# Two of sixteen tiles' neighbour coordinates by indirect DMA on GpSimd in place of lookups by matrix product

## The chip, the cores and the metric

The kernel runs on one core of a Trainium2 chip. The metric is the device time of one execution in microseconds (us), the median of several runs.

## What is computed

There are B = 2 samples with N = 1024 points. Each point has C = 512 features in `x` and 1024 coordinates in `ctx`. Two layers follow each other.

```python
# layer 0: 8 nearest neighbours in ctx, four blocks (w_center = w_neighbor = w = fside)
idx = top_k(-squared_distance(ctx), 8)
for i in range(4):
    shortcut = points
    p = leaky_relu(points, 0.01)
    g = gather(p, idx)
    points = (w[i] @ p + (w[i] @ g).sum(neighbours)) / 9 + shortcut
# layer 1: 30 nearest neighbours in ctx, features from the first three coordinates only
idx = top_k(-squared_distance(ctx), 30)
rel = ctx[first three][idx] - ctx[first three][own]
feat = spherical(rel), and the same less its mean           # 6 per neighbour
h = lrelu(bn(feat @ W1.T)); h = lrelu(bn(h @ W2.T)); h = lrelu(bn(h @ W3.T))   # 6, 3, 1
att = softmax(h, over 30 neighbours)
out = x + sum_k att[k] * x[idx[k]]
```

`bn` normalises with the mean and the variance over all points of both samples, so no point of layer 1 is through it before the coordinates of the neighbours of all 2048 points are there.

## The kernel before

**Tiles and passes.** The 2048 points are 16 tiles (`TILES`) of 128; tiles 0 to 7 are the first sample. The four blocks of layer 0 are eight passes, `it` = 0 to 7, the samples in turn. A pass has sixteen steps, numbered through as g = 16 it + s. Steps 0 to 7 are the aggregation half: a unit of work (`aggregate`, L1447 to L1468) is 16 matmuls of 128x512, adjacency `nbr` against the high and the low part of the features. The first two units of a pass are issued together, their matmuls alternating (a double step), and both end with it. Steps 8 to 15 are the product half (`wp`, L1470 to L1490), 12 matmuls each, with the weights `wT` in a high and a low part.

**What stands behind a unit.** Each aggregation unit leaves a bank that ACT copies (`q_high`, L719) and from which DVE makes the low part (`q_low`, L994). PE wants the low part of a unit before the third one behind it, since there are three banks (`s_ql`). Each product step is added to `X` by DVE (`x_update`, L1000). GpSimd (POOL in the profile) makes the next pass's features in product steps: `p_join` (L496) and `p_low` (L501). In pass 2 it also makes four low parts of the second half of the weights (`w_low`, L460), which the product half of pass 2 waits for.

**Order.** Each engine has a program of its own. PE, ACT and DVE do, after their part of step g, what `side(g)` has for it; GpSimd has a loop of its own over the same steps (L547 to L571), without a wait for the step itself. Layer 1 lies in these places:

- `SEL_AT`: the selection of the 30 neighbours on DVE, to step 43 (pass 2). It leaves `idx`, the neighbours' numbers. Tiles 0 and 1 are the first and stand ahead of pass 0.
- `ROWS_AT` = steps 30, 33, 36, 44: `index_rows` (L1004 to L1013), four small DVE operations that split the numbers of four tiles into a row and a place in it. PE turns them, and SP writes them to DRAM and reads them back broadcast over 128 partitions, one DMA for each lookup (L380 to L397).
- Lookups, from `G0` = 44: a lookup `u` is 15 neighbours of the 128 points of a tile, so 32 in all, two in a step. DVE and ACT turn the broadcast numbers into one-hots (L1017, L732), PE multiplies them with a table of coordinates in three bf16 parts (`lookup`, L1500 to L1515: 45 matmuls of 128x24), and DVE's `pick_r` (L1020 to L1031) takes the wanted one of eight in each group of 24 and writes it to `near`. They lie in steps 45 to 61 on PE.
- `NET_AT`: 47 steps of the small network from `M0` = G0 + TILES + 2 = 62 on, mostly DVE and ACT over all 61,440 neighbours at once. In some of them PE sums statistics over the partitions (L1519).
- `T0` = 109: the attention weights are turned (L1241 to L1245 on DVE make their parts). From `S0` = T0 + 6 = 115 on DVE makes one-hots (`onehots`, L1257 and L1266), and PE multiplies them two times a step into rows of a 128 x 1024 matrix of weights (`spread`, L1573, 64-column matmuls), the first one ahead of the unit of step S0 + 1. `S_END` of these 32 spreads lie inside pass 7; the others, and the weighted sum itself (`attend`, L1612 to L1614), come behind it.

On SP the own-coordinate loads (L360) take single elements: 1024 of them for a coordinate of a sample.

## Time and profile before

| | |
|---|---|
| median of 3 runs | 716.52 us (716.1 to 717.33) |
| the profiled execution | 717.41 us |
| its span in the trace | 715.7 us, so 1.7 us outside |
| PE busy | 699.1 us (98% of the span) |
| DVE busy | 576.3 us (81%) |
| ACT busy | 347.9 us (49%) |
| GpSimd busy | 249.9 us (35%) |
| granted TensorE clock, mean | 0.995 of full speed |

Matmuls are pipelined: a row gives 0.39 us for a large one though the next starts 0.227 us later. So a busy share of 98% does not say that PE is at its best; distances between starts do. The trace gives times from the start of the span. A row of a timeline has the start, the duration, the engine, the line, the operation with its operands, how many like it follow each other, and, in brackets, how long the engine stood idle before and what released it.

### The profile page before, as it was taken

What the parts mean: (1) busy time and instruction counts of PE and PEld (TensorE: products, weight loads), DVE (VectorE), ACT (ScalarE), POOL (GpSimd) and SP (SyncE); (2) the same over time, 40 slices, a digit from 0 to 9 for tenths busy, and PEclk for the clock granted to TensorE, in tenths of its full rate; (3) what the DMA queues carried; (4) which work ended last, traced back from release to release, by engine and by line L of the source; (5) the groups of instructions that cost most, each with busy time, mean ns of one, the idle gap of its engine ahead of it and who ended that gap; (6) DMA issues with size and microseconds to landing.
All of it is one profiled execution on the core that took longest, in us unless ns stands there. A gap on an engine that the chain in (4) does not pass through costs nothing.

```text
span 715.7 us, 13026 instructions
## 1 busy us (share of the span) xinstructions
PE 699.1 (98%) x5458; PEld 584.2 (82%) x5458; DVE 576.3 (81%) x848; ACT 347.9 (49%) x526; POOL 249.9 (35%) x216
## 2 busy tenths in 40 slices
PE   5999999999999999999999999999999999999998
PEld 4799889778888887888888888877887887888887
DVE  4699999999699899766789798677686799678831
ACT  6456646448517137767892263384463244223210
POOL 2258757656608327300165083065074000000000
PEclk9999999999999999999999999999999999999999
DMA  8510301100000103645510000000000000100101
GB/s 350 182 3 1 117 1 37 53 29 1 1 1 0 62 24 141 200 154 163 179 38 1 1 0 1 0 1 1 0 1 0 2 1 2 45 32 32 45 30 60
DMA packets 21564, 35.66 MB, mean 50 GB/s; under 512 B 10113, under 2 KB 10369, under 8 KB 21505
## 3 DMA queue, kind: packets, MB, share of 16 engines
q1 hardware_dynamic: 20976, 33.78, 14.2%
q10 hardware_dynamic: 528, 1.05, 0.4%
q8 instruction: 43, 0.70, 0.4%
q14 instruction: 17, 0.13, 0.1%
HBM read 30.50 MB, written 4.33 MB: 49 GB/s over the span
## 4 chain that ended last, share of the span: by engine, by line
PE 81%; DVE 9%; POOL 4%; ACT 3%; issue 1%; DMA 1%; SPq 0%; POOLq 0%; DVEq 0%
PE bank L1464 27%; PE bank L1486 7%; PE bank L1488 6%; PE bank L1487 6%; PE bank L1511 5%; PE bank L1573 4%; PE bank L1612 4%; PE bank L1614 4%; PE bank L1375 4%; PE bank L1613 4%; PE bank L1377 4%; PE bank L1376 4%; DVE idx L967 2%; DVE vals L965 2%; POOL pts_l L430 1%
## 5 line engine op out<-in xcount | busy, mean ns | idle before, releaser
L1464 PE MATMUL bank<-nbr,pts_h 128*128 128x512 f32 x512 | 202.7, 396 | 1.5 <-DVE pts_l L994 1.4
L1464 PE MATMUL bank<-nbr,pts_l 128*128 128x512 f32 x512 | 200.0, 391 | 0.0
L496 POOL TENSOR_TENSOR p_second<-p_first,p_second 128x512 f32<-128x512 f32 x58 | 76.9, 1329 | 196.9 <-ACT p_second L706 196.9
L1464 PEld LDWEIGHTS bank<-nbr,pts_h 128*128 128x128 f32 x512 | 96.6, 189 | 23.1 <-issue 2.1
L719 ACT CAST pts_h<-bank 128x512 fp32r<-128x512 f32 x64 | 37.1, 587 | 159.4 <-PE bank L1464 159.2
L1464 PEld LDWEIGHTS bank<-nbr,pts_l 128*128 128x128 f32 x512 | 96.6, 189 | 19.7 <-issue 0.2
L1486 PE MATMUL bank<-wT,pts_h 128*128 128x512 f32 x256 | 102.2, 399 | 0.0
L1488 PE MATMUL bank<-wT,pts_l 128*128 128x512 f32 x256 | 100.3, 392 | 0.0
L1487 PE MATMUL bank<-wT,pts_h 128*128 128x512 f32 x256 | 100.1, 391 | 0.0
L994 DVE TENSOR_TENSOR pts_l<-bank,pts_h 128x512 fp32r<-128x512 f32 x64 | 44.0, 688 | 48.8 <-ACT pts_h L719 48.4
L501 POOL TENSOR_TENSOR pts_l<-p_second,pts_h 128x512 fp32r<-128x512 f32 x58 | 78.3, 1356 | 2.0 <-ACT pts_h L712 2.0
L1375 PE MATMUL bank<-pts_h 128*128 128x512 f32 (+3 forms) x192 | 68.8, 358 | 8.8 <-DVE pts_l L927 8.3
L837 ACT CAST nbr<-bank 128x512 fp32r<-128x512 f32 x64 | 35.2, 590 | 78.3 <-PE bank L1573 78.3
L1376 PE MATMUL bank<-pts_l,pts_h 128*128 128x512 f32 (+3 forms) x192 | 66.1, 344 | 0.0
L1377 PE MATMUL bank<-pts_h,pts_l 128*128 128x512 f32 (+3 forms) x192 | 66.1, 344 | 0.0
L1488 PEld LDWEIGHTS bank<-wT,pts_l 128*128 128x128 f32 x256 | 48.3, 189 | 10.3
L1486 PEld LDWEIGHTS bank<-wT,pts_h 128*128 128x128 f32 x256 | 48.5, 189 | 9.5
L1487 PEld LDWEIGHTS bank<-wT,pts_h 128*128 128x128 f32 x256 | 48.5, 189 | 9.5
L712 ACT CAST pts_h<-p_second 128x512 fp32r<-128x512 f32 x58 | 35.7, 616 | 31.2 <-POOL p_second L496 31.2
L1000 DVE SCALAR_TENSOR_TENSOR X<-bank,X 128x512 f32<-128x512 f32 x64 | 43.9, 689 | 7.8 <-PE bank L1488 7.2
L1612 PE MATMUL bank<-pts_h,nbr 128*128 128x512 f32 x120 | 48.7, 406 | 0.6 <-DVE pts_l L1275 0.6
L1375 PEld LDWEIGHTS bank<-pts_h 128*128 128x128 f32 x192 | 36.6, 191 | 13.7 <-issue 7.3
(212 smaller groups left out, 1338.4 us busy)
## 6 DMA issues: line engine op xcount, KB each, us to landing
more<-a_rows SPq DMA_DIRECT2D x17, 480.0 KB, 4.5
scratch<-a_rows SPq DMA_DIRECT2D x15, 480.0 KB, 4.7
X<-in_ctx SPq DMA_DIRECT2D x12, 512.0 KB, 6.1
out_dram<-X SPq DMA_DIRECT2D x15, 256.0 KB, 2.0
more<-in_ctx SPq DMA_DIRECT2D x4, 512.0 KB, 5.6
X<-in_x SPq DMA_DIRECT2D x2, 1024.0 KB, 5.2
X<-in_x SPq DMA_DIRECT2D x1, 1536.0 KB, 7.0
w_raw<-in_fside_BxSxS SPq DMA_DIRECT2D x1, 1024.0 KB, 11.5
```

The source lines that it names most:

```text
L496: pool.tensor_tensor(p, a, b, ALU.subtract).then_inc(s_p32, 1)
L501: pool.tensor_tensor(p_l[:, m, :], parts(n)[2], p_h[:, m, :].bitcast(F32), ALU.subtract).then_inc(s_p1, 1)
L994: dve.tensor_tensor(q_l[:, j, :], bank[g % 3][:], q_h[:, j, :].bitcast(F32), ALU.subtract).then_inc(s_ql, 1)
L1000: dve.scalar_tensor_tensor(dst, bank[3 + g % 3][:], 1.0 / (K0 + 1.0), dst, ALU.mult, ALU.add).then_inc(s_xu, 1)
L1375: pe.matmul(o, pts_h[:, k, rows], pts_h[:, k, cols], start=(k == 0), stop=False)
L1376: pe.matmul(o, pts_h[:, k, rows], pts_l[:, k, cols], start=False, stop=False)
L1377: return pe.matmul(o, pts_l[:, k, rows], pts_h[:, k, cols], start=False, stop=(k == KT - 1))
L1464: mm = pe.matmul(bank[u % 3][:], p[:, m, t * P:(t + 1) * P], nbr[b][:, m, hf * HALF:(hf + 1) * HALF], start=(m == 0 and part_ == 0), stop= ...
L1486: pe.matmul(bank[3 + g % 3][:], q_h[:, q, cols], wT[:, hi, t, :], start=(t == 0), stop=False)
L1487: pe.matmul(bank[3 + g % 3][:], q_h[:, q, cols], wT[:, 1 - hi, t, :], start=False, stop=False)
L1488: mm = pe.matmul(bank[3 + g % 3][:], q_l[:, q, cols], wT[:, hi, t, :], start=False, stop=(t == CT - 1))
L1612: pe.matmul(o, lhs[0], rhs[0], start=(r == 0), stop=False)
```

## The change

`GATHERED_TILES` = 2. The coordinates of the neighbours of tiles 0 and 1 no longer come from lookups. Three DMAs on SP write the first three coordinates of the first sample into a DRAM table of 1024 rows, point by point. GpSimd then issues 60 indirect DMAs, one for each tile and neighbour: each reads 128 numbers from `idx` and fetches 128 rows of three coordinates into `near_rows`. `GATHER_AT` places them in the first halves of passes 1, 2 and 3: 16, 16 and 28. Ahead of the network's first step DVE waits for all 60 and copies them into `near`.

28 lookups stay, those of tiles 2 to 15, still two a step from step 45 on. Since `M0` follows their number, the network starts at step 60 and not 62, `T0` is 107 and `S0` 113, and four more spreads lie inside pass 7 (`S_END` 30 and not 26).

```diff
+    GATHERED_TILES = 2
+        near_rows = sb("near_rows", [P, GATHERED_TILES, K1, 3], F32)
+        tab_d = nc.dram_tensor("table", [N, 3], F32, kind="Internal").ap()
+        GT = GATHERED_TILES
+        LOOKUPS = 2 * (TILES - GT)
...
-        M0 = G0 + TILES + 2
+        M0 = G0 + LOOKUPS // 2 + 2
+        GATHER_AT = {16: 2, 17: 2, 18: 2, 19: 2, 20: 2, 21: 2, 22: 2, 23: 2, 32: 3, 33: 3, 34: 3, 35: 3, 36: 1, 37: 1, 38: 1,
+                     39: 1, 48: 4, 49: 4, 50: 4, 51: 4, 52: 3, 53: 3, 54: 3, 55: 3}
...
+            for j in range(3):
+                sp.dma_start(tab_d[:, j].unsqueeze(1), ctx[0, 2 - j, :].unsqueeze(1),
+                             allow_slow_non_contiguous=True).then_inc(s_tabd, 16)
...
             for c in range(CHUNKS):
-                for t in range(2 * CH):
-                    u = 2 * CH * c + t
+                for t in range(2 * CH) if c else range(2 * GT, 2 * CH):
+                    u = 2 * CH * c + t - 2 * GT
...
+                    done = sum(GATHER_AT[q] for q in GATHER_AT if q < g)
+                    for i in range(done, done + GATHER_AT.get(g, 0)):
+                        if i == 0:
+                            pool.wait_ge(s_tabd, 16 * 3)
+                            pool.wait_ge(s_sel, GT)
+                        pool.indirect_dma_start(
+                            out=near_rows[:, i // K1, i % K1, :], out_offset=None, in_=tab_d,
+                            in_offset=bass.IndirectOffsetOnAxis(ap=idx[:, i // K1, i % K1:i % K1 + 1], axis=0)) \
+                            .then_inc(s_rows, 16)
...
-                if 0 <= g - G0 < TILES:
+                if 0 <= g - G0 < LOOKUPS // 2:
                     onehot_a(2 * (g - G0) + 1)
...
             def pick_r(u):
-                T, k0 = u // 2, (u % 2) * KH
+                T, k0 = GT + u // 2, (u % 2) * KH
...
                 if n == 0:
+                    dve.wait_ge(s_rows, 16 * GT * K1)
+                    link(dve.tensor_copy(near[:, :, 0:GT, :], near_rows[:].rearrange("p t k j -> p j t k")))
...
-                    if 0 <= u < 2 * TILES:
+                    if 0 <= u < LOOKUPS:
...
-                b = u // (2 * NT)
+                b = (GT + u // 2) // NT
```

What moves on GpSimd in passes 1 and 2. Before, the four low parts of the weights (L460) of pass 2 stand right behind the features made in pass 1 (L496, L501; `x2` means two in a row):

```order
L496 TENSOR_TENSOR p_second<-p_first,p_second 128x512
L501 TENSOR_TENSOR pts_l<-p_second,pts_h 128x512 x2
L460 TENSOR_TENSOR wT<-w_raw,wT 128x512 x4
L496 TENSOR_TENSOR p_second<-p_first,p_second 128x512 x2
L501 TENSOR_TENSOR pts_l<-p_second,pts_h 128x512
```

With the change (L511 and L516 are the features, L475 the low parts):

```order
L511 TENSOR_TENSOR p_second<-p_first,p_second 128x512
L516 TENSOR_TENSOR pts_l<-p_second,pts_h 128x512 x2
L579 DMA near_rows<-table,idx 128x3 x12
L475 TENSOR_TENSOR wT<-w_raw,wT 128x512
L579 DMA near_rows<-table,idx 128x3
L475 TENSOR_TENSOR wT<-w_raw,wT 128x512
L579 DMA near_rows<-table,idx 128x3
L475 TENSOR_TENSOR wT<-w_raw,wT 128x512
L579 DMA near_rows<-table,idx 128x3
L475 TENSOR_TENSOR wT<-w_raw,wT 128x512
L579 DMA near_rows<-table,idx 128x3
L511 TENSOR_TENSOR p_second<-p_first,p_second 128x512 x2
```

Twelve gathers now stand ahead of the first low part of the weights, and one behind each of the four.

What moves on DVE at the passes 6 and 7. Before, the parts of the turned weights (L1241 to L1245) end ahead of pass 7, three low parts of its aggregation (`q_low`, L994) follow, and then one-hots 0 (L1257 twice, L1266):

```order
L1241 CAST more<-scratch 128x512x2
L1242 TENSOR_TENSOR more<-scratch,more 128x512x2
L1243 TENSOR_TENSOR scratch<-bank,scratch 128x512
L1244 CAST more<-scratch 128x512x2
L1245 TENSOR_TENSOR more<-scratch,more 128x512x2
L994 TENSOR_TENSOR pts_l<-bank,pts_h 128x512 x3
L1257 TENSOR_TENSOR scratch<-scratch 128x512
L1257 TENSOR_TENSOR scratch<-idx,scratch 128x2048
L1266 TENSOR_TENSOR scratch<-scratch,more 128x2048
L994 TENSOR_TENSOR pts_l<-bank,pts_h 128x512
```

With the change (L1267 to L1271 the parts, L1024 the product steps of pass 6, L1018 `q_low`, L1283 and L1292 one-hots 0):

```order
L1267 CAST more<-scratch 128x512x2
L1268 TENSOR_TENSOR more<-scratch,more 128x512x2
L1269 TENSOR_TENSOR scratch<-bank,scratch 128x512
L1270 CAST more<-scratch 128x512x2
L1271 TENSOR_TENSOR more<-scratch,more 128x512x2
L1024 SCALAR_TENSOR_TENSOR X<-bank,X 128x512 x2
L1018 TENSOR_TENSOR pts_l<-bank,pts_h 128x512
L1283 TENSOR_TENSOR scratch<-scratch 128x512
L1283 TENSOR_TENSOR scratch<-idx,scratch 128x2048
L1292 TENSOR_TENSOR scratch<-scratch,more 128x2048
L1018 TENSOR_TENSOR pts_l<-bank,pts_h 128x512
```

The parts now end two product steps ahead of pass 7, and one-hots 0 stand behind its first low part and not its third; on PE the first spread stands behind the double step of pass 7 and ahead of its third unit.

## Rows read from the trace of the kernel before

**Rows 1.** The page, chain that ended last: share of the span by engine.
```profile
PE 81%; DVE 9%; POOL 4%; ACT 3%; issue 1%; DMA 1%; SPq 0%; POOLq 0%; DVEq 0%
```
**Rows 2.** The chain in order of time: start us, us, engine, line and count.
```profile
352.08 2.27 PE bank L1511 x90
357.19 2.27 PE bank L1511 x90
...
433.80 29.03 PE bank L1464 x128
```
**Rows 3.** Own-coordinate loads: SP's queue in the timeline; the page's DMA issues (landing).
```profile
38.58 0.43 SPq L360 DMA_DIRECT2D own<-in_ctx  x1
...
own<-in_ctx SPq DMA_DIRECT2D x6, 4.0 KB, 2.3
```
**Rows 4.** Timeline of GpSimd, passes 1 to 3.
```profile
218.04 2.56 POOL L496 TENSOR_TENSOR p_second<-p_first,p_second 128x512 f32<-128x512 f32 x2 [25.66 <-ACT p_second L706]
...
235.60 2.54 POOL L501 TENSOR_TENSOR pts_l<-p_second,pts_h 128x512 fp32r<-128x512 f32 x2
254.07 1.29 POOL L460 TENSOR_TENSOR wT<-w_raw,wT 128x512 fp32r<-128x512 f32 x1 [15.92 <-ACT wT L579]
...
265.09 1.29 POOL L460 TENSOR_TENSOR wT<-w_raw,wT 128x512 fp32r<-128x512 f32 x1 [2.43 <-ACT wT L579]
...
352.36 1.27 POOL L496 TENSOR_TENSOR p_second<-p_first,p_second 128x512 f32<-128x512 f32 x1 [53.72 <-ACT p_second L706]
```
**Rows 5.** Timeline of PE: the first normalisation sum, and the start of pass 6.
```profile
471.49 0.39 PE L1519 MATMUL bank<-stat,mean_mat 128*128 128x12 f32 x2 [0.52 <-DVE stat L1073]
...
490.66 0.39 PE L1464 MATMUL bank<-nbr,pts_l 128*128 128x512 f32 x1
...
492.63 0.40 PE L1464 MATMUL bank<-nbr,pts_l 128*128 128x512 f32 x1
```
**Rows 6.** Timelines of ACT, DVE and PE at the start of pass 7.
```profile
545.70 1.08 ACT L719 CAST pts_h<-bank 128x512 fp32r<-128x512 f32 x2 [3.57 <-PE bank L1464]
549.78 0.59 ACT L719 CAST pts_h<-bank 128x512 fp32r<-128x512 f32 x1 [3.00 <-PE bank L1464]
...
550.40 0.69 DVE L994 TENSOR_TENSOR pts_l<-bank,pts_h 128x512 fp32r<-128x512 f32 x1 [1.40 <-ACT pts_h L719]
...
553.80 0.39 PE L1573 MATMUL bank<-scratch 128*128 128x64 bf16 x8 [0.43 <-issue]
```
**Rows 7.** Timeline of PE: an idle in pass 0, and matmuls in pass 2.
```profile
146.70 0.47 PE L1464 MATMUL bank<-nbr,pts_h 128*128 128x512 f32 x1 [1.44 <-DVE pts_l L994]
...
288.19 0.63 PE L1487 MATMUL bank<-wT,pts_h 128*128 128x512 f32 x1
288.62 0.63 PE L1488 MATMUL bank<-wT,pts_l 128*128 128x512 f32 x1
```
**Rows 8.** Busy us of each engine (operations) by windows; granted clock; DMA share; GB/s.
```profile
283.40:287.00 3.60, 2.27 (x70) 1.84 (x69) 3.60 (x6) 2.50 (x3) 1.33 (x2) 1.00 0.99 370
287.00:290.40 3.40, 3.40 (x36) 2.82 (x33) 3.23 (x8) 3.40 (x5) 0.82 (x1) 0.50 0.90 285
...
310.90:314.30 3.40, 3.40 (x49) 2.92 (x46) 3.23 (x8) 3.37 (x3) 0.00 (x0) 0.50 0.83 260
```
**Rows 9.** Timeline of DVE in pass 2: index rows, a `q_low`, a one-hot.
```profile
237.04 1.19 DVE L1009 TENSOR_SCALAR scratch<-idx 128x128 uint32<-128x128 uint32 x1
...
245.50 0.69 DVE L994 TENSOR_TENSOR pts_l<-bank,pts_h 128x512 fp32r<-128x512 f32 x1 [1.83 <-ACT pts_h L719]
...
249.69 0.22 DVE L1009 TENSOR_SCALAR scratch<-idx 128x128 uint32<-128x128 uint32 x1
...
282.23 1.36 DVE L1012 CAST scratch<-scratch 128x128 bf16<-128x128 uint32 x1
283.51 1.74 DVE L1017 TENSOR_SCALAR scratch<-scratch,part 128x1920 bf16<-128x1920 bf16 x1
```
**Rows 10.** Timeline of PE: the first product matmul of pass 2.
```profile
267.30 0.39 PE L1486 MATMUL bank<-wT,pts_h 128*128 128x512 f32 x1
```

More of the change, by code:

```diff
@@ L249, in build @@
         s_tab = sem("table_ready")
+        s_tabd = sem("table_stored")
+        s_rows = sem("neighbour_rows_landed")
         s_first = sem("first_term_ready")
@@ L389, in _ @@
                         sp.dma_start(a_rows[CHUNKS - 1], a_row[:]).then_inc(s_arow, 16)
-                    if u == 2 * CH * (CHUNKS - 1):
+                    if u == 2 * CH * (CHUNKS - 1) - 2 * GT:
                         sp.wait_ge(s_arow, 16 * CHUNKS)
@@ L1282, in side @@
                     index_rows(ROWS_AT[g])
-                if 0 <= g - G0 < TILES:
+                if 0 <= g - G0 < LOOKUPS // 2:
                     onehot_a(2 * (g - G0))
                 for u in (2 * (g - G0) - 4, 2 * (g - G0) - 3):
-                    if 0 <= u < 2 * TILES:
+                    if 0 <= u < LOOKUPS:
                         pick_r(u)
@@ L1529, in side @@
                 for u in (2 * (g - G0) - 2, 2 * (g - G0) - 1):
-                    if 0 <= u < 2 * TILES:
+                    if 0 <= u < LOOKUPS:
                         lookup(u)
```

## Prediction

> **What bounds the kernel now.** I read the chain that ended last first: PE holds 81% of it [rows 1]. Then I read PE's own timeline, where the reader should look at the distances between starts and not at the busy shares. Large matmuls start 0.227 us apart nearly everywhere: 29.03 us for the 128 of an aggregation half [rows 2], so 3.63 us for an aggregation step of sixteen and 2.72 us for a product step of twelve. Behind the selection PE is the bound and rarely waits; what leaves its queue is a gain, and what makes it idle is a loss that nothing later repays. The exceptions are therefore what matters: the start of the lookups (283 to 314 us), the normalisation sums (471 and 491 us) and the first spread (553.8 us).
>
> **What is removed.** Four of 32 lookups, two steps with two each. A pair of lookups is 90 small matmuls in 2.27 us, and product steps that carry one start 5.11 us apart, from 352.08 to 357.19 [rows 2], against 2.72 without. Steps 60 and 61, both product steps, lose it: 2 x (5.11 - 2.72) = **4.8 us less on PE**, straight on the bound. ACT, DVE and SP lose the one-hots, reads and broadcasts of these lookups; none of them is on the bound there, so I count nothing.
>
> **What is added on queues.** Three table stores on SP: the nearest row is the own-coordinate load, also 1024 single elements, 0.43 us to issue and 2.3 us to land [rows 3]. They stand right behind those loads, and the reader is GpSimd at 192 us (218.04 less 25.66 [rows 4]): nothing. Sixty gathers on GpSimd: no row shows one. From below it is an issue of 0.43 us, from above a full landing, 2.3 us [rows 3]; I take 1.3 us, what GpSimd needs for one of its own operations (two in 2.54 us at 235.60 [rows 4]), since both are work over 128 rows on that engine. GpSimd does not wait for the steps of the table, so each batch begins when its queue is free. Pass 1: 16 x 1.3 = 20.8 us into an idle stretch of 25.66 us that ends at 218.04. Pass 2: 12 x 1.3 = 15.6 us into 15.92 us, before the first low weight part at 254.07, then one gather after each of the four parts, which start 3.7 us apart (254.07 to 265.09) and take 1.3. Pass 3: 28 x 1.3 = 36.4 us into 53.72 us [rows 4]. All fits, barely in pass 2, and costs nothing as long as a gather is no dearer. The copy of 180 elements on DVE at step 60 lies where PE does not wait for DVE: nothing.
>
> The Trainium skill (DMA: Bandwidth & Descriptors, Latency and other measured facts) gives about 1 us to the first byte of a DMA issued from GpSimd; no run shows one here yet. By that page twelve would be an estimated 12 us, and the sum is the same.
>
> **What is moved.** The network, the turning of the weights and the spreads all start two steps earlier.
>
> First the two waits that the network now causes. At 471.49 PE stood 0.52 us for the first sum's statistics, in the third product step of pass 5, behind a backlog of DVE work that does not fit 2.72 us steps. At 490.66 to 492.63, the start of pass 6, six starts took 1.97 us where 1.36 would do: 0.6 us for late low parts, since six normalisations on ACT held them up [rows 5]. Two steps earlier the heavy items before the sum fall in aggregation steps of 3.6 us, and the normalisations come before more of the product half: I take both waits as gone, **-1.1 us**. New ones of the same kind may appear (the second sum now follows the pass's double step, and the weights' parts are made beside the low parts of pass 7): 0 to 1 us, **+0.5 us**, by the 0.52 and 0.6 of these rows.
>
> Then the first spread, the term that decides. Before, one-hots 0 stand on DVE three `q_low` into pass 7 and PE wants them after four aggregation units; PE idled 0.43 us [rows 6]. Now they stand after the first `q_low`, and PE wants them right behind the double step that opens the pass. In that double step the two units alternate and end together, so no unit of work lies between. From the copy on ACT that follows a unit to the spread it took 553.80 - 549.78 = 4.02 us (copy, then 3.40 us from `q_low` through the one-hots [rows 6]). The copy after the double step started at 545.70, so the spread could start at 549.72; PE is through with the pair two matmuls after that copy is released, at 546.15. Idle 3.6 us in place of 0.43: **+3.1 us**, and nothing behind it has room to give it back.
>
> Does the clock fall in such a hole? It stayed at full speed after the one idle of 1.44 us at 146.70: the matmul behind it took 0.47 us, and not the 0.63 of those at the lower level [rows 7]. It was granted 0.50, the 1.2 GHz level, for 3.4 us twice, at 287.0 after 3.6 us of waiting and small matmuls, and at 310.9 [rows 8]; large matmuls then started 0.43 us apart, 288.19 to 288.62 [rows 7]. 3.6 us of pure idle is nearer to the second kind. 3.4 us hold eight matmuls at 0.2 us extra each, 1.6 us; a part falls on the spread's small ones: **+1.4 us**, with 0 and 1.7 as ends.
>
> **The sum.** -4.8 - 1.1 + 0.5 + 3.1 + 1.4 = -0.9 us on the profiled execution's 717.41, so 716.5 us. That execution is 0.9 us above the median of the runs, 716.52; I carry the difference over to the median: **715.6 us**, -0.13%. A measurement of this kernel can tell about 0.2%, 1.4 us, from no change.
>
> **Rivals.**
>
> 1. *Gathers hold up DVE (slower).* GpSimd's operations do hold up some of DVE's: the shift at 237.04 took 1.19 us, 0.22 us at 249.69 when GpSimd was idle [rows 9]; the selection's searches show nothing of the kind. If a gather does the same, the index rows suffer. They are chains of four small operations, and in the gap between two the next gather starts. At 238 us three of them wait 1.3 us each, 3.9, of which the idle 1.83 us at 245.50 [rows 9] takes back all but 2.1. The second chain then starts at 251.8, and the batch runs to about 254: two waits, 2.6. The third may meet a low part and a gather, 0 to 2.5. DVE has no idle from 245.50 until it starts the lookups, so this moves PE's wait there: 4.7 to 7.2 us, less 1 to 2 if the present collisions (1.36 us for a cast at 282.23, 1.74 for the one-hot behind it [rows 9]) fall away. I take +3: **718.6 us**; the ends are 1 (gathers of 0.8 us) and 6. It is slower than before from 0.9 us up, more than the measurement's grain from 2.3. Against it: a gather reads 128 indices and may hold the memory port shortly. The Trainium skill (SBUF — State Buffer, SBUF: two separate sides) calls the port pair that DVE and GpSimd share an exclusive lock, held for a whole instruction, and says that GpSimd writes its descriptors through it; the slow shift agrees for arithmetic, no run shows a gather.
>
> 2. *The clock holds (faster).* Without the fall and without new small waits: -4.8 - 1.1 + 3.1 = -2.8, **713.7 us**. For it: the idle of 146.70 passed without one. Against: this one is two and a half times as long.
>
> 3. *The hole is not there (faster).* If DVE had one-hots 0 ready in time: -4.8 - 1.1 + 0.5 = -5.4, **711.1 us**. The order of the queue speaks against it.
>
> 4. *The gathers don't fit, so that they are not hidden as meant.* At 2.3 us the twelve of pass 2 end near 266, 11.7 us after the first low weight part was due, and the product that needs the last one starts at 267.30 [rows 10]: PE late by 10 us, **726 us** or more. It begins to cost above about 1.6 us a gather.
>
> **How the numbers follow.** Forecast 0.42, rival 1 0.33, rival 2 0.14, rival 3 0.05, rival 4 0.06. Range 712.9 to 720.0: it leaves out rivals 3 and 4 and the dear end of rival 1 (0.05), together 0.16. Faster by over 0.2% (below 715.1): 0.11 of the forecast, whose terms are good to about 1 us, 0.13 of rival 2, 0.05 of rival 3, 0.01 of rival 1: 0.30. Slower by over 0.2% (above 718.0): 0.20 of rival 1, 0.06 of rival 4, 0.01 of the forecast: 0.27. Within: 0.43.
>
> **What the profile of the changed kernel would show.** Product steps 60 and 61 start 2.72 us apart. Before the first 64-column matmul of pass 7 PE idles some 3.6 us, and the granted clock is 0.50 for a few us behind it; if it is not, rival 2. PE's waits at the first sum and at the start of pass 6 are gone. Index rows in pass 2 take 0.9 us a chain as now; if their operations take over 1 us each and the first lookup starts later against the step's other work, rival 1. GpSimd's gathers end before 254 and leave the low weight parts where they are; otherwise rival 4. Wrong would be above all a hole at the first spread that is shorter than 2 us, or a first lookup more than 1 us later.

## The result: 3.3% slower, and where the time went

The changed kernel takes 739.41 us in the median of 5 runs (739.12 to 743.68), the kernel before 716.79 us beside it: 1.0329 of its time, 95% interval 1.0311 to 1.0346, so 22.6 us slower. The forecast was 715.6 us. The profiled execution is the longest of the five, 743.68 us with a span of 741.9, and the table below is made on it; its mean granted clock is 0.972, that of the four others 0.975 to 0.977.

The chain of the changed kernel, by engine, shows the first sign. "issue", time in which an engine waits for nothing that the profile shows, was 1% in [rows 1]:

```profile
PE 80%; DVE 9%; POOL 4%; issue 4%; ACT 2%; DMA 1%; POOLq 0%; SPq 0%
```

The second view to make is a table by half passes: the distance in PE's timeline from the first large matmul of one half to that of the next, in us. Halves that are not listed agree within 0.04 us.

| half | before | after |
|---|---|---|
| pass 2, product | 31.84 | 30.51 |
| pass 3, aggregation | 49.97 | 76.93 |
| pass 3, product | 33.76 | 29.00 |
| pass 5, product | 22.79 | 22.01 |
| pass 6, aggregation | 29.89 | 29.86 |
| pass 7, aggregation | 34.43 | 42.96 |
| pass 7, product, and the end | 142.64 | 140.49 |

So 27.0 us more in one half, and about what was forecast in the others. (Pass 2's 1.3 us is the clock: before, it fell there [rows 8], this time not.) In pass 3 GpSimd's 28 gathers run from 299.35 to 340.77 us, the first four from beside the large matmuls of the double step, most of the others beside lookups. From their timeline; they start 1.25 us apart, and behind every seventh GpSimd pauses:

```profile
311.07 0.95 POOL L579 DMA_INDIRECT near_rows<-table,idx  x1 [0.30 <-issue]
312.32 0.94 POOL L579 DMA_INDIRECT near_rows<-table,idx  x1 [0.30 <-issue]
315.19 0.95 POOL L579 DMA_INDIRECT near_rows<-table,idx  x1 [1.93 <-issue]
...
339.83 0.94 POOL L579 DMA_INDIRECT near_rows<-table,idx  x1 [0.30 <-issue]
```

And PE's timeline beside them (the small matmuls of the lookups, the number behind x, and in brackets the idle time before):

```profile
305.05 1.29 PE L1537 MATMUL bank<-tab_p,more 128*128 128x24 bf16 x45
306.19 0.27 PE L1537 MATMUL bank<-tab_p,scratch 128*128 128x24 bf16 x5
306.84 0.29 PE L1537 MATMUL bank<-tab_p,scratch 128*128 128x24 bf16 x5 [0.38 <-issue]
307.62 0.25 PE L1537 MATMUL bank<-tab_p,scratch 128*128 128x24 bf16 x4 [0.49 <-issue]
309.05 0.28 PE L1537 MATMUL bank<-tab_p,scratch 128*128 128x24 bf16 x5 [1.18 <-issue]
...
314.82 1.30 PE L1537 MATMUL bank<-tab_p,scratch 128*128 128x24 bf16 x38 [0.52 <-issue]
316.56 0.31 PE L1537 MATMUL bank<-tab_p,scratch 128*128 128x24 bf16 x5 [0.44 <-issue]
...
348.30 2.43 PE L1537 MATMUL bank<-tab_p,more 128*128 128x24 bf16 x90
```

Fifty matmuls run at full pace. Then they come in handfuls, some 0.72 us or twice that from one to the next, in the middle of a lookup: its 45 matmuls wait for semaphores only ahead of the first. At the end of GpSimd's pause (between the rows of 312.32 and 315.19) 38 run freely, and then it starts again. After the last gather a pair takes 2.3 us as in [rows 2]. Behind these gaps the granted clock was 0.50 for a time (the third figure from the end of these rows):

```profile
314.80:316.20 1.40, 1.30 (x38) 1.15 (x37) 0.80 (x2) 0.00 (x0) 0.95 (x1) 0.50 0.72 244
327.70:333.30 5.60, 5.60 (x16) 4.44 (x16) 0.00 (x0) 0.00 (x0) 4.08 (x6) 0.50 0.08 16
```

The lower clock does not make the handfuls, since the 38 free ones ran at it, in 1.30 us. Piece by piece against the same half of the kernel before: the four lookups behind the double step take 22.66 us (305.05 to 327.71) where they took 5.36, the unit behind them 6.37 for 4.88, the next pair of lookups 8.35 (334.08 to 342.43) for 2.28, and the unit behind that 5.87 for 3.74. 17.3 + 1.5 + 6.1 + 2.1 is the 27.0 us; the two units are longer by the clock. One line of the waits from 299 to 342 us sums it up: who waited, for whom, us in total, times, longest. Before:

```profile
PE bank L1511 <- issue: 0.2, 1, 0.2
```

After:

```profile
PE bank L1537 <- issue: 18.5, 30, 1.2
```

The first spread of pass 7, which answers to [rows 6], and the window behind it, with a granted clock of 0.50, which answers to [rows 8]:

```profile
570.33 1.01 PE L1599 MATMUL bank<-scratch 128*128 128x64 bf16 x16 [3.58 <-issue]
571.15 0.77 PE L1490 MATMUL bank<-nbr,pts_h 128*128 128x512 f32 x1
```

```profile
568.90:575.70 6.80, 5.37 (x27) 4.43 (x28) 4.53 (x6) 0.59 (x1) 0.00 (x0) 0.50 0.00 0
```

And the first normalisation sum, [rows 5], now without an idle ahead of it:

```profile
486.11 0.29 PE L1545 MATMUL bank<-stat,mean_mat 128*128 128x12 f32 x2
```

### The profile page after: what moved, and what is told of

It reads as the page before. It is cut to its first block, busy times and chain, and to the rows that moved or that the text cites. A ratio compares the mean times of both kernels' runs of the same rounds, so it can differ in the third digit from the quotient of the medians.

```text
span 741.9 us, 12697 instructions
## 1 busy us (share of the span) xinstructions
PE 705.4 (95%) x5278; PEld 586.8 (79%) x5278; DVE 571.7 (77%) x835; ACT 341.1 (46%) x522; POOL 309.0 (42%) x276
## 4 chain that ended last, share of the span: by engine, by line
PE 80%; DVE 9%; POOL 4%; issue 4%; ACT 2%; DMA 1%; POOLq 0%; SPq 0%
PE bank L1490 27%; PE bank L1512 6%; PE bank L1514 6%; PE bank L1513 6%; PE bank L1537 5%; PE bank L1599 4%; PE bank L1638 4%; PE bank L1640 4%; PE bank L1401 4%; PE bank L1639 4%; PE bank L1403 4%; PE bank L1402 4%; DVE idx L991 2%; DVE vals L989 2%; POOL pts_l L445 1%
## 5 line engine op out<-in xcount | busy, mean ns | idle before, releaser
L1490 PE MATMUL bank<-nbr,pts_h 128*128 128x512 f32 x512 | 206.6, 403 | 1.7 <-DVE pts_l L1018 1.5
L1490 PE MATMUL bank<-nbr,pts_l 128*128 128x512 f32 x512 | 203.4, 397 | 0.0
L511 POOL TENSOR_TENSOR p_second<-p_first,p_second 128x512 f32<-128x512 f32 x58 | 78.9, 1363 | 150.4 <-ACT p_second L730 150.4
L1490 PEld LDWEIGHTS bank<-nbr,pts_h 128*128 128x128 f32 x512 | 98.8, 193 | 24.3 <-issue 2.1
L1490 PEld LDWEIGHTS bank<-nbr,pts_l 128*128 128x128 f32 x512 | 98.8, 193 | 20.3 <-issue 0.2
L1018 DVE TENSOR_TENSOR pts_l<-bank,pts_h 128x512 fp32r<-128x512 f32 x64 | 43.8, 684 | 50.1 <-ACT pts_h L743 49.6
L516 POOL TENSOR_TENSOR pts_l<-p_second,pts_h 128x512 fp32r<-128x512 f32 x58 | 78.4, 1356 | 2.0 <-ACT pts_h L736 2.0
L579 POOL DMA_INDIRECT near_rows<-table,idx x60 | 57.4, 957 | 29.5 <-issue 29.0
L1024 DVE SCALAR_TENSOR_TENSOR X<-bank,X 128x512 f32<-128x512 f32 x64 | 43.4, 682 | 6.1 <-PE bank L1514 5.4
```

The source lines that it names most:

```text
L511: pool.tensor_tensor(p, a, b, ALU.subtract).then_inc(s_p32, 1)
L516: pool.tensor_tensor(p_l[:, m, :], parts(n)[2], p_h[:, m, :].bitcast(F32), ALU.subtract).then_inc(s_p1, 1)
L579: pool.indirect_dma_start(out=near_rows[:, i // K1, i % K1, :], out_offset=None, in_=tab_d, in_offset=bass.IndirectOffsetOnAxis(ap=idx[:, ...
L1018: dve.tensor_tensor(q_l[:, j, :], bank[g % 3][:], q_h[:, j, :].bitcast(F32), ALU.subtract).then_inc(s_ql, 1)
L1490: mm = pe.matmul(bank[u % 3][:], p[:, m, t * P:(t + 1) * P], nbr[b][:, m, hf * HALF:(hf + 1) * HALF], start=(m == 0 and part_ == 0), stop= ...
```

## Experiments: is it the gathers, and which?

My theory after the result (A): while GpSimd issues gathers, PE's instructions come slowly, some 53 in the 8.5 us from 306.3 to 314.8 (matmuls and their weight loads). About a hundred wait in PE when it starts, the 50 matmuls that still ran freely. Large matmuls take 8.8 instructions a microsecond, so they live on what waits until GpSimd pauses; lookups take 80 and run dry. The rivals that I named: the moved network and spreads (B), and the memory port that DVE shares with GpSimd, my rival 1 (C).

**e1: only the 28 gathers of pass 3, everything else as before.** The gathers of pass 3 of the change's diff are added to the kernel before, and nothing reads their rows:

```diff
+        GATHER_AT = {48: 4, 49: 4, 50: 4, 51: 4, 52: 3, 53: 3, 54: 3, 55: 3}
```

> The kernel before, with all 32 lookups, plus the table and only the 28 gathers of pass 3 (their rows are not used). Theory A, PE is short of instructions while GpSimd issues gathers: in the changed kernel's trace PE gets some 9 instructions per 0.72 us between 306 and 342 us, enough for large matmuls (2 per 0.227 us, 6.3 per 0.72 us) and far too few for lookups (2 per 0.025 us); so the four lookups of the double step and the pair behind it stretch by about 24 us here too: 738 to 743 us. Theory B, the loss comes with what was moved (network, spreads, fewer lookups): 717 us. Theory C, GpSimd holds the port that DVE's one-hots and reads need: later one-hots, 719 to 725 us, with idle time of PE put down to DVE and none inside a lookup.

737.37 us, 1.0284 (1.0269 to 1.0300) of the kernel before. The aggregation half of pass 3 took 73.53 us, every other half as before, and PE's waits there read

```profile
PE bank L1530 <- issue: 17.0, 26, 1.2
```

That is just under A's 738 to 743. So the gathers alone make a loss of that size, and B falls; of C there is nothing, since DVE waits for PE and not PE for DVE.

**e2: only the 32 gathers of passes 1 and 2.**

```diff
+        GATHER_AT = {16: 2, 17: 2, 18: 2, 19: 2, 20: 2, 21: 2, 22: 2, 23: 2, 32: 3, 33: 3, 34: 3, 35: 3, 36: 1, 37: 1, 38: 1, 39: 1}
```

> The kernel before, with all 32 lookups, plus the table and only the 32 gathers of passes 1 and 2 (their rows are not used). Theory A: PE has only large matmuls there, so no loss, 716 to 718 us. Theory C (my rival 1, gathers hold up the index rows): 718 to 722 us with index rows of over 1 us each. If gathers cost PE in proportion to their number wherever they stand: 740 us.

717.03 us, 0.9992 (0.9977 to 1.0008). All 32 gathers, of the same length, beside large matmuls cost nothing. The group of gathers (busy us and mean ns of one); then one gather, two operations of an index row beside it in DVE's timeline, and the second of them in the kernel before:

```profile
L573 POOL DMA_INDIRECT near_rows<-table,idx x32 | 30.6, 956 | 14.6 <-issue 14.4
```

```profile
249.77 0.95 POOL L573 DMA_INDIRECT near_rows<-table,idx  x1 [0.30 <-issue]
249.82 0.23 DVE L1028 CAST scratch<-scratch 128x128 f32<-128x128 uint32 x1
250.34 0.42 DVE L1030 CAST scratch<-scratch 128x128 bf16<-128x128 uint32 x1
```

```profile
250.47 0.23 DVE L1012 CAST scratch<-scratch 128x128 bf16<-128x128 uint32 x1
```

Beside a gather one operation of this index row takes 0.42 us in place of 0.23. So a gather can hold DVE for some 0.2 us, not for the 1.3 of my rival 1, and the run as a whole shows no cost of it.

**e4: plain DMAs of the same size in place of e1's gathers.**

```diff
-                        pool.indirect_dma_start(
-                            out=near_rows[:, i // K1, i % K1, :], out_offset=None, in_=tab_d,
-                            in_offset=bass.IndirectOffsetOnAxis(ap=idx[:, i // K1, i % K1:i % K1 + 1], axis=0)) \
-                            .then_inc(s_rows, 16)
+                        pool.dma_start(near_rows[:, i // K1, i % K1, :], tab_d[(i % 8) * P:(i % 8 + 1) * P, :]).then_inc(s_rows, 16)
```

> As e1, but the 28 DMAs of GpSimd in pass 3 are plain ones of the same 128 x 3 elements, without an index. If any DMA that GpSimd issues starves PE of instructions, the stretch is as in e1 for as long as they last (some 20 to 35 us): 730 to 743 us. If it is the reading of indices alone: 717 us.

715.92 us, 0.9992 (0.9982 to 1.0003), and the waits of PE read 0.2 us as before. GpSimd issues seven in a row, 0.56 us each, and the lookups beside them run at full pace:

```profile
307.06 4.01 POOL L573 DMA_DIRECT2D near_rows<-table  x7 [4.38 <-issue]
...
307.72 1.28 PE L1527 MATMUL bank<-tab_p,scratch 128*128 128x24 bf16 x45
309.18 1.28 PE L1527 MATMUL bank<-tab_p,scratch 128*128 128x24 bf16 x45 [0.18 <-issue]
```

Both kinds move 32 packets a DMA, on the same queue (`q0 software_dynamic: 896, 0.04, 0.2%` on both pages). So the transfers are not the cause, nor that GpSimd issues a DMA: it is the indirect form.

**e5: a lookup of 15 matmuls and not 45.** It leaves out the two lower parts of the coordinates.

```diff
-                    for i in range(3):
+                    for i in range(1):
                         mm = pe.matmul(bank[6 + u % 2][:, k * 3 * AB:(k + 1) * 3 * AB],
                                        bc[u % NB][:, k * P:(k + 1) * P],
                                        tab_p[:, i, b].rearrange("p j r -> p (j r)"),
-                                       start=(i == 0), stop=(i == 2))
+                                       start=(i == 0), stop=True)
```

> The changed kernel with 15 matmuls in a lookup and not 45: the two lower bf16 parts of the coordinates are left out, so this computes less. Without any stretch the aggregation half of pass 3 would be 29.0 + 8 x 0.76 = 35 us. Theory A (PE's supply of instructions falls to some 9 per 0.72 us, with about 100 waiting in PE when a lookup starts, as in the changed kernel's trace, where the first 51 matmuls with their weight loads still ran at full speed): the four lookups of the double step are 120 instructions, about all of which already wait, so 35 to 39 us. If each small matmul is slow by itself beside gathers (180 of them took 22.8 us, 0.1 us more each): 35 + 8 = 43 us. If PE can't run small matmuls at all until the gathers end at 341 us: over 60 us. The whole: 694 to 702 us, since 28 lookups also lose 0.75 us each.

710.85 us, 0.9904 (0.9889 to 0.9920), where I had expected 694 to 702. The half took 48.14 us, which no theory had: with lookups this short PE waits for the one-hots instead, and the granted clock is 0.50 in three stretches of 3.4 us. But the matmuls themselves ran as A says: the four lookups of the double step, 120 instructions, at full pace, and one lookup later in handfuls. So a small matmul is not slow by itself beside gathers.

```profile
307.35 0.52 PE L1537 MATMUL bank<-tab_p,scratch 128*128 128x24 bf16 x15 [1.70 <-DVE more L1041]
...
323.92 0.36 PE L1537 MATMUL bank<-tab_p,scratch 128*128 128x24 bf16 x8
324.55 0.23 PE L1537 MATMUL bank<-tab_p,scratch 128*128 128x24 bf16 x3 [0.27 <-issue]
325.27 0.17 PE L1537 MATMUL bank<-tab_p,scratch 128*128 128x24 bf16 x1 [0.50 <-issue]
```

**e10, e10_again: gathers beside spreads.** 28 gathers, added to the kernel before from the start of pass 7 on; each partition fetches the row of its own number.

```diff
+        GATHER_AT = {16 * (ITS - 1): 28}
...
+                            pool.wait_ge(s_wm, NT * (ITS - 1))
+                        pool.indirect_dma_start(
+                            out=near_rows[:, i // K1, i % K1, :], out_offset=None, in_=tab_d,
+                            in_offset=bass.IndirectOffsetOnAxis(ap=idx0[:, 0:1], axis=0)) \
+                            .then_inc(s_rows, 16)
```

> The kernel before, all 32 lookups, with 28 gathers (each partition fetches the row of its own number; the rows are not used) that GpSimd issues from the start of pass 7, 538.6 us, on: some 41 us, beside the first units of large matmuls and then beside the spreads, 64 matmuls of 64 columns a step. Theory A is about PE's instructions and not about lookups: no loss up to the first spread at 553.8 us; then a step of 16 large matmuls and 64 small ones, 160 pairs' halves of which few are waiting, gets some 9 instructions per 0.72 us with breaks, so each of the two or three steps until 580 us grows by 5 to 9 us: 727 to 742 us, with gaps inside the spreads that no engine ends. If it is the lookups' own operands (one-hots, table of coordinates) that collide: 716 to 718 us.

720.42 us in the median, 1.0044 (1.0025 to 1.0064), but from 715.94 to 723.14, and the profiled execution was the shortest: no gap at all. I had counted 128 small instructions a step; it is 64, so a step wants 20 a microsecond and not 34. A's 727 to 742 us were missed by that. By A, 20 are just past what comes in and waits together, and the price, 0 to 6 us, would hang on where GpSimd's pauses fall; no run shows this. The same kernel once more:

> The kernel of e10 once more, for a second profiled execution. Its timed executions took 715.9 to 723.1 us. Theory A: an execution that takes more than 718 us shows gaps inside the spreads of pass 7 that no engine ends, and a pass 7 longer by the difference; if the time lies elsewhere (another pass, outside the span), the gathers beside spreads are not what costs.

719.31 us; the aggregation half of pass 7 took 37.32 us in place of 34.45. One gap stands inside a spread, a longer one ahead of another:

```profile
563.01 0.19 PE L1597 MATMUL bank<-scratch 128*128 128x64 bf16 x1 [0.46 <-issue]
569.45 0.63 PE L1597 MATMUL bank<-scratch 128*128 128x64 bf16 x16 [1.39 <-issue]
```

```profile
568.13 1.22 DVE L1290 TENSOR_TENSOR scratch<-scratch,more 128x2048 bf16<-128x2048 bf16 x1
```

Only the first is what A means. At the second PE waits, in spite of "issue", for one-hots that DVE ends at 569.35. DVE was late because it heard late of an earlier spread: its last matmul ended at 562.03, and DVE went on at 566.65.

**e11 against e12: denser spreads, with and without gathers.** In both each spread has 40 matmuls; e11 has e10's gathers, e12 none.

```diff
+                    for _ in range(3):
+                        pe.matmul(bank[6 + q % 2][:, n * 2 * KP:(n + 1) * 2 * KP], oa[q // 2 % 2][:, m],
+                                  mv[q // 2 % 2][:, m, 0:2].rearrange("p h r -> p (h r)"), start=True, stop=True)
                     for i in range(2):
```

> As e10 (28 gathers from the start of pass 7), but each spread has 40 matmuls and not 16: the first half's are issued four times, the same values again. A step of pass 7 then holds 192 instructions of PE in about 6.3 us. Theory A, with a queue of about 100 and some 53 instructions in the 8.5 us of seven gathers: a cycle of 10.4 us gives about 150, and would want 300; over the 40 us of gathers beside spreads some 15 to 25 us are lost against e12, with gaps inside the spreads. If only the lookups' operands matter: within 4 us of e12.

> The kernel before with the same spreads of 40 matmuls and no gathers: the comparison for e11. 32 spreads x 24 more matmuls x about 0.033 us = 25 us more than before: 735 to 750 us by every theory.

779.53 us against 760.67, so 18.9 us for the gathers, inside A's 15 to 25; e12 itself took some 10 us more than the top of what I had reckoned. All of it lies in one half, pass 7's aggregation, 59.85 against 40.74 us. In e11 the first two spreads still run through, and then it is the pattern of the lookups:

```profile
560.82 0.22 PE L1597 MATMUL bank<-scratch 128*128 128x64 bf16 x2 [0.29 <-issue]
...
561.58 0.20 PE L1597 MATMUL bank<-scratch 128*128 128x64 bf16 x1 [0.45 <-issue]
562.29 0.19 PE L1597 MATMUL bank<-scratch 128*128 128x64 bf16 x1 [0.51 <-issue]
...
563.75 0.23 PE L1597 MATMUL bank<-scratch 128*128 128x64 bf16 x1 [1.15 <-issue]
```

Other operands, other weights, another place in the program, and rows in order in place of neighbours: so it is not what a lookup reads. What the lookups and these spreads share is how many instructions a microsecond PE wants while gathers are issued.

**What A leaves out: PE's signals come late too.** In the changed kernel the last of the first lookup's 45 matmuls ends at 306.34 (305.05 and 1.29). DVE, which stands ready to read the result, starts 7.9 us later, in GpSimd's pause; in the kernel before it starts 0.7 us behind the matmuls (307.80) and without a wait. (`remote`: the profile ties the signal to no instruction that had just ended.)

```profile
314.22 0.53 DVE L1050 TENSOR_TENSOR scratch<-bank,scratch 128x360 f32<-128x360 f32 x1 [7.23 <-remote]
```

```profile
308.48 0.53 DVE L1026 TENSOR_TENSOR scratch<-bank,scratch 128x360 f32<-128x360 f32 x1
```

In e10's profiled execution, where PE has no gap, two spreads end at 557.60, and ACT's copy of the second waits 2.0 us longer:

```profile
556.49 1.11 PE L1597 MATMUL bank<-scratch 128*128 128x64 bf16 x32
```

```profile
559.59 0.59 ACT L861 CAST nbr<-bank 128x512 fp32r<-128x512 f32 x1 [1.72 <-remote]
```

A slow supply of instructions does not say that a signal is late when PE is on time. So more than the supply is slowed, or PE stops because its finished work is reported too slowly; no run tells these apart. Beside the large matmuls of e2's passes 1 and 2, ACT's copies start 0.03 to 0.04 us behind the unit where ACT waits for it, but for one at 0.77.

## Experiments: can the change be saved?

**e3 and e3b: one gathered tile, none beside lookups.** e3 is the changed kernel with `GATHERED_TILES = 1` and its 30 gathers in passes 1 and 2. In e3b the spreads also start where they did before the change.

```diff
-    GATHERED_TILES = 2
+    GATHERED_TILES = 1
...
-        S0 = T0 + 6
+        S0 = T0 + 7
```

> The changed kernel with GATHERED_TILES = 1 and its 30 gathers all in passes 1 and 2, none beside lookups; 30 lookups, network one step earlier than before. Theory A: the stretch of pass 3 is gone; one product step loses its pair (-2.4 us), the first spread stands one unit later than in the changed kernel, so its hole is 0 to 3 us and not 4: 713.5 to 717 us. If gathers cost wherever they stand: over 725 us.

> One tile gathered, all 30 gathers in passes 1 and 2, and the spreads at S0 = 115 as before the change. In the run of one tile pass 7's aggregation half and the end took 36.82 + 141.56 us against 34.43 + 142.64 before: 1.3 us lost. Theory: these come back, 713.7 us. If the earlier spread costs nothing here: 715.0 us.

e3: 715.01 us, 0.9973 (0.9960 to 0.9986). e3b: 714.85 us, 0.9962 (0.9948 to 0.9975). Both are a little faster than the kernel before. The intervals overlap, and pass 7 with the end takes 178.38 and 178.22 us: the 1.3 us did not come back. With one unit of work between the double step and the first spread PE idles 0.52 us ahead of it, hardly more than before [rows 6]; what both lose is at the opening of pass 7, 1.3 us between two starts. PE waits there for GpSimd's features of this pass; while DVE makes the parts of the turned weights, an operation of GpSimd that takes 1.28 us elsewhere takes 2.27. In e3:

```profile
536.13 2.27 POOL L510 TENSOR_TENSOR p_second<-p_first,p_second 128x512 f32<-128x512 f32 x1
```

```profile
542.37 0.50 PE L1489 MATMUL bank<-nbr,pts_h 128*128 128x512 f32 x1 [0.94 <-POOL pts_l L515]
```

**e6: the spreads where they were, the gathers untouched.**

```diff
-        S0 = T0 + 6
+        S0 = T0 + 8
```

> The changed kernel with the spreads where they were before the change (S0 = 115), gathers untouched. My step on the first spread: the hole of 4 us ahead of it and the clock's fall behind it go, the rest stays: pass 7's aggregation half 34.4 us as before, and 739.4 - 6 = 733 us. If hole and clock were an after-effect of pass 3 or of the earlier network: no change, 739 us.

731.64 us, 1.0196 (1.0181 to 1.0212). The idle ahead of the first spread is 0.43 us again, the clock stays up, and pass 7 with the end takes 177.82 us and not 183.45: 5.6 us for the hole and the clock together. The wait for GpSimd's features at the opening stays. Pass 3 is still at 71.35 us.

**e7: all 60 gathers, but paced.** 34 in passes 1 and 2, the rest behind a wait for the lookups of the step before, so that they fall beside large matmuls; S0 = T0 + 8.

```diff
+        GATHER_AT = {16: 3, 17: 2, 18: 2, 19: 2, 20: 2, 21: 2, 22: 2, 23: 2, 32: 3, 33: 3, 34: 3, 35: 3, 36: 1, 37: 1, 38: 1,
+                     39: 2, 45: 1, 46: 2, 47: 1, 48: 4, 50: 2, 51: 2, 52: 2, 53: 2, 54: 2, 55: 2, 56: 1, 57: 1, 58: 1, 59: 3}
+        LOOKED_AT = {g: 2 * (g - 1 - G0) for g in GATHER_AT if g > G0 + 1}
...
+                    if g in LOOKED_AT:
+                        pool.wait_ge(s_look, LOOKED_AT[g])
```

> The changed kernel with all 60 gathers, but paced: 34 in passes 1 and 2, and the 26 others from step 45 to 59, each behind a wait of GpSimd for the lookups of the step before, so that they run beside large matmuls; the spreads at S0 = 115. Theory A: PE's queue is full again when the next lookups start, so the stretch is gone: aggregation half of pass 3 at 48 to 51 us, 716.8 - 4.8 (two pairs) - 0.8 (first sum) = 711 us, 709.5 to 713. If 60 gathers cost PE in some other way (the number of DMAs, DVE's copy, the network's earlier place): over 716 us.

725.61 us, 1.0115 (1.0099 to 1.0130), and not the 709.5 to 713 of A. The aggregation half of pass 3 is at 49.79 us and PE's waits for "issue" back at 0.2 us: pacing does what A says. But the product half behind it took 40.77 us in place of 29.00. DVE's timeline and GpSimd's there:

```profile
369.00 12.38 DVE L1146 COPY scratch<-near_rows 128x180 f32<-128x180 f32 x1 [1.65 <-DMA near_rows<-table,idx]
381.42 2.04 DVE L1062 TENSOR_TENSOR scratch<-scratch,own 128x480 f32<-128x480 f32 x3
...
367.59 1.31 POOL L512 TENSOR_TENSOR p_second<-p_first,p_second 128x512 f32<-128x512 f32 x1
368.83 1.31 POOL L517 TENSOR_TENSOR pts_l<-p_second,pts_h 128x512 fp32r<-128x512 f32 x1
...
378.74 2.48 POOL L517 TENSOR_TENSOR pts_l<-p_second,pts_h 128x512 fp32r<-128x512 f32 x2
```

The copy that I had counted at nothing is 180 elements and took 12.38 us. Behind the three gathers of step 59 GpSimd's eleven operations from 367.59 on follow each other without a gap to 381.22, and DVE's copy ends 0.16 us behind the last. `x_update` stands behind it on DVE, and PE waited 9.5 us for that. The Trainium skill (SBUF — State Buffer, SBUF: two separate sides) says that the pair of ports which DVE and GpSimd share is held for a whole instruction. The end of the copy agrees with one blocking the other, but here it lasted over ten instructions in a row.

**e9a, e9b, e9c: three ways round it.** e9a lets ACT make the copy; e9b leaves it on DVE and moves the gathers of step 59 to steps 56 to 58; e9c does both.

```diff
-                    dve.wait_ge(s_rows, 16 * GT * K1)
-                    link(dve.tensor_copy(near[:, :, 0:GT, :], near_rows[:].rearrange("p t k j -> p j t k")))
+                    dve.wait_ge(s_ncopy, 1)
...
+                if g == M0 - 1:
+                    act.wait_ge(s_rows, 16 * GT * K1)
+                    act.copy(near[:, :, 0:GT, :], near_rows[:].rearrange("p t k j -> p j t k")).then_inc(s_ncopy, 1)
...
-                     39: 2, 45: 1, 46: 2, 47: 1, 48: 4, 50: 2, 51: 2, 52: 2, 53: 2, 54: 2, 55: 2, 56: 1, 57: 1, 58: 1, 59: 3}
+                     39: 2, 45: 1, 46: 2, 47: 1, 48: 4, 50: 2, 51: 2, 52: 2, 53: 2, 54: 2, 55: 2, 56: 2, 57: 2, 58: 2}
```

> As e7 (60 paced gathers), but the gathered rows are copied by ACT and not by DVE. In e7 that copy of 180 elements took 12.38 us on DVE (369.00 to 381.42), over just the time in which GpSimd worked without a gap, and PE waited 9.5 us for DVE behind it. Theory D: the copy needs what GpSimd holds while it works back to back; on ACT it takes under 1 us, and pass 3's product half goes from 40.77 to 29 to 33 us (DVE's three subtractions behind it may still be held up): 713 to 718 us. If the late gathers themselves (three at step 59, landing at 369) are the cause: 723 to 726 us as e7.

> As e7, with DVE's copy, but no gathers at step 59: two each at steps 56 to 58. So GpSimd is not behind when the copy comes, and its operations leave gaps. Theory D: the copy takes under 2 us, product half of pass 3 at 29 to 31 us, 713 to 715 us. If the copy's own wait for the rows was the loss: the same gain, so this run alone does not tell the two apart, but e9a does. If gathers beside the lookups of steps 56 to 58 starve PE again: over 720 us.

> Both: ACT copies, and no gathers at step 59. Theories A and D: product half of pass 3 at 29.0 us as in the changed kernel, aggregation half 49.8, first sum without its wait, pass 7 as in e6: 716.8 - 4.8 - 0.8 + 0.7 = 712 us, 711 to 713.5, faster than the kernel before and than one gathered tile.

712.92, 712.32 and 712.78 us: 0.9955 (0.9940 to 0.9971), 0.9941 (0.9926 to 0.9956) and 0.9952 (0.9938 to 0.9965). The copy, on ACT in e9a and on DVE in e9b, the latter with GpSimd's operations beside it:

```profile
369.65 0.43 ACT L801 COPY scratch<-near_rows 128x180 f32<-128x180 f32 x1 [5.75 <-DMA near_rows<-table,idx]
```

```profile
368.86 0.64 DVE L1146 COPY scratch<-near_rows 128x180 f32<-128x180 f32 x1
```

```profile
368.05 1.30 POOL L512 TENSOR_TENSOR p_second<-p_first,p_second 128x512 f32<-128x512 f32 x1
369.30 1.31 POOL L517 TENSOR_TENSOR pts_l<-p_second,pts_h 128x512 fp32r<-128x512 f32 x1
```

The product half is 29.52, 29.00 and 29.00 us. So the late gathers were not the loss by themselves (e9a has them), the 12.38 us of the copy on DVE were. Why it took so long in e7 is open. A GpSimd without gaps is not enough: in e9b too, and around the 0.64 us of the copy in the changed kernel, one operation of GpSimd follows the other, and the copy gets through where one ends. In e7, other than there, DVE had first stood idle for the gathered rows (1.65 us), and the copy began 0.17 us into an operation of GpSimd (368.83 to 369.00); no run tests either. All three beat both kernels, by 3 to 4 us against the kernel before, and are not told apart among themselves.

## Why the prediction was wrong, point by point

- **What is removed: right.** Pass 3's product half is 4.76 us shorter; 4.8 was the term.
- **The gathers on GpSimd's queue: right, and beside the point.** 0.95 us and 0.30 of idle, 1.25 us apart (1.3 taken), and behind every seventh an idle of 1.8 to 2.0 us in place of the 0.30, which I did not have. The sixteen of pass 1 end at 215.94 of 218; the first low weight part starts at 254.62 and not 254.07. All fit, as the step said. The table's stores took 10.5 us to land and not 2.3, long before the first gather at 192.83.
- **The step that failed** is the sentence behind it: "All fits, barely in pass 2, and costs nothing as long as a gather is no dearer." I asked what a gather takes from GpSimd's queue, from SP and from DVE's port, and never what PE does beside it. 28 gathers beside lookups cost 27 us in the profiled execution, and e1 gives 20.3 us for them alone. None of the rivals had it. Rival 1 named the wrong engine, and e2 shows 0.2 us of it; rival 4 asks for gathers that are too long, and they were not. On the page the place could be seen: PE wants 2 instructions per 0.025 us in a lookup, and GpSimd's idle stretch of 53.72 us, where I put 28 gathers, is that of the lookups [rows 2, 4]. No row of the trace before could have given the price, since none shows a gather; that was a reason for a wider range, with the 28 gathers beside lookups as its dear end.
- **The network's waits: half right.** The one ahead of the first sum is gone, with 0.78 us in pass 5's product half (0.52 taken). The 0.6 us at the start of pass 6 stayed, 29.86 against 29.89 us: the six normalisations are not what holds the low parts up there, or not they alone; no run tests it further.
- **New small waits, +0.5: about right.** 0.7 us at the opening of pass 7 in e6, though the wait there is for GpSimd's features beside the weights' parts, and not for DVE's low parts.
- **The first spread: right, the size of the clock's fall wrong.** Start to start 3.98 us where it was 0.81, so +3.2 for +3.1. The clock then stayed at its lower level for 6.8 us and not 3.4. e6 gave 5.6 us back; less the 3.2 of the hole, that leaves about 2.4 for the clock, where I took 1.4 with 1.7 as the dear end.
- **The copy at step 60, counted at nothing**, took 0.64 us in the changed kernel, and 12.38 in e7. The reason I gave, that PE does not wait for DVE there, was the weak one: `x_update` stands behind it.

Without the stretch of pass 3 the sum was good: 743.68 - 27.0 = 716.7 us for the profiled execution, where it gave 716.5. That it comes so near is luck in part: pass 7 and the end are 6.4 us longer where the sum had 5.0, and pass 2's 1.3 us at full clock, which no term had, took that back.

What is shown: the loss comes from indirect gathers beside dense small matmuls, with lookups (e1) and with spreads (e11), not from plain DMAs (e4), not beside large matmuls (e2), and not when paced (e7, e9). That the slow thing is the supply of PE's instructions is a reading: it fits the numbers of e5 and e11, and e10's only afterwards, and it does not account for PE's late signals. By which path a gather on GpSimd slows PE is open. The transfers that bring instructions do not show it: the pages have `q8 instruction: 43, 0.70, 0.4%` before and `q8 instruction: 42, 0.69, 0.4%` after, the same share of the DMA engines' time. The Trainium skill (the same page and section) says that engines' ports and DMAs' are separate and that, of the engines' ports, only the pair of DVE and GpSimd makes anyone wait. PE's gaps beside indirect DMAs (18.5 us) do not fit a reading of that as a promise for PE's pace.

## What to carry to other kernels

Before work is put into an idle stretch of an engine, look at what the other engines do in it, PE's instructions per microsecond among it: beside large matmuls these gathers were free, beside 24-column ones each cost 0.7 to 1.0 us of PE. If such work must run there, let it wait for the dense part to end; that took the 27 us out of pass 3's half, and with the spreads at their old place and the copy short again it left a gain of 3 to 4 against the kernel before. And look at the length of a small operation that you move beside GpSimd's work, and at who stands behind it: ACT made the copy in 0.43 us where DVE had needed 12.38.

## What the runs showed of the hardware that I had not expected

- While GpSimd issues indirect DMAs of 128 rows, PE runs small matmuls in handfuls some 0.72 us apart, 53 instructions in 8.5 us, after about 100 at full pace; with plain DMAs it does not.
- Beside them PE's signals to other engines come late: 7.9 us at a lookup of the changed kernel, 2.0 us in e10 though PE had no gap.
- GpSimd issues seven DMAs and then pauses: 1.8 to 2.0 us behind indirect ones (in the changed kernel), 4.1 to 5.6 us behind plain ones, which take 0.56 us each.
- A copy of 128 x 180 elements on DVE lasted through ten operations of GpSimd in a row in one kernel, 12.38 us, and took 0.64 to 0.80 beside such a row in six others.
